# A transformer block with 16 sequences on one core: the last two turns get their own order of dense groups

## What is computed

```python
def _L0_attn_ref(x, Wqkv, bqkv, Wo, bo):
    kqv = (x @ Wqkv + bqkv).reshape(b, s, 3, NUM_HEADS, HEAD_SIZE)   # 16 heads of 32
    ...
    attn = jax.nn.softmax(scores, axis=2)                            # causal
    ...
    return out @ Wo + bo

def _router(x, router_w, e_bias):        # 32 experts, 3 of 8 groups, then 4 of 32 for each token
    ...
def _moe_forward(...):
    topk_idx, topk_w = _router(x, router_w, e_bias)
    # every (token, choice) gets a position within its expert, in token order over all 8192 tokens;
    # positions under C = 320 are kept: slots_token, slots_w
    ...
    Xp = x[slots_token].reshape(E, C, d)                             # 32 experts x 320 tokens
    Y = jnp.einsum('eci,eid->ecd', jax.nn.silu(G) * U, W_down)
    out = jnp.zeros((T, d), x.dtype).at[slots_token].add(Yf)
    shared = jax.nn.silu(x @ shared_gate.T) * (x @ shared_up.T) @ shared_down.T

x = x + _L0_attn_ref(_layernorm(x), ...)
x = x + _L0_ffn_ref(_layernorm(x), ...)
```

## Time and profile before

| what | us |
|---|---|
| median of 3 runs | 2513.14 (2513.05, 2513.14, 2518.89) |
| profiled execution: its time | 2517.61 |
| profiled execution: its span | 2515.8 |
| PE busy in the span | 2311.3 (92%) |
| DVE busy | 1573.3 (63%) |
| ACT busy | 1083.8 (43%) |
| POOL busy | 1110.4 (44%) |

### The profile page before, as it was taken

One profiled execution on the slowest core, in us unless ns is written; L12 is line 12 of the kernel. 1 busy time (PEld: TensorE's weight loads), 2 busy tenths in 40 slices (PEclk: granted clock), 3 DMA queues, 4 the chain that ended last, 5 costly groups with the idle time before them and its releaser, 6 DMA issues. The chain is left out here.

```text
span 2515.8 us, 48721 instructions
## 1 busy us (share of the span) xinstructions
PE 2311.3 (92%) x15466; PEld 1159.8 (46%) x15466; DVE 1573.3 (63%) x4870; ACT 1083.8 (43%) x1849; POOL 1110.4 (44%) x1622
## 2 busy tenths in 40 slices
PE   3789999999999999999999999999998985999997
PEld 1334444444444444444444444444443443666664
DVE  4355666675766666666666666666666564666664
ACT  3344444444343434343434443434443313666664
POOL 1223244434343434444444444444443354777775
PEclk8889999999999999999999999999998897999999
DMA  4212222222222222222222222222212016888886
GB/s 166 68 43 60 53 69 58 67 55 72 57 66 61 65 67 57 66 69 61 60 61 60 60 60 60 60 60 60 62 41 76 10 55 184 230 233 238 236 234 121
DMA packets 180850, 222.52 MB, mean 88 GB/s; under 512 B 37776, under 2 KB 119792, under 8 KB 180624
## 3 DMA queue, kind: packets, MB, share of 16 engines
q1 hardware_dynamic: 154000, 177.58, 23.7%
q0 software_dynamic: 26624, 42.12, 7.5%
HBM read 112.65 MB, written 56.46 MB: 67 GB/s over the span
## 5 line engine op out<-in xcount | busy, mean ns | idle before, releaser
L917 DVE CUSTOM_DVE_ANT_0 junk<-scores,maskrow 128x512 f16<-128x512 f32 (+3 forms) x1024 | 462.5, 487 | 198.2 <-PE scores L524 130.8
L650 ACT ACTIVATE probs<-scores_T 128x512 f32<-128x512 f32 x640 | 369.6, 598 | 215.8 <-PE scores_T L539 212.9
L1033 POOL TENSOR_SCALAR_AFFINE_SELECT probs<-probs 128x256 f32<-128x256 f32 x512 | 192.6, 413 | 380.8 <-ACT probs L650 379.9
L539 PE MATMUL scores_T<-stack_q,stack_k 97*128 97x512 f16 (+3 forms) x1024 | 251.9, 308 | 53.3 <-ACT probs L650 42.7
L1042 POOL DMA_INDIRECT slots_dram<-rec,idx x256 | 258.8, 1011 | 89.0 <-issue 80.1
L524 PE MATMUL scores<-stack_k,stack_q 96*128 96x512 f16 (+3 forms) x1024 | 253.7, 310 | 44.6 <-DVE nmax L917 41.0
L172 PE MATMUL dense<-xT_hi,wqkv_hi 128*128 128x512 f16 x512 | 196.1, 383 | 1.5 <-DVE xT_lo L888 1.5
L173 PE MATMUL dense<-xT_lo,wqkv_hi 128*128 128x512 f16 x512 | 195.0, 381 | 0.0
L174 PE MATMUL dense<-xT_hi,wqkv_lo 128*128 128x512 f16 x512 | 194.9, 381 | 0.0
L1019 POOL TENSOR_TENSOR xres<-xres,bo 128x512 f32<-128x512 f32 x64 | 81.2, 1268 | 247.3 <-DMA xres<-in_x 247.3
L1159 POOL DMA_INDIRECT out<-ex_y,ex_sidx x96 | 153.3, 1597 | 76.6 <-issue 39.1
(11 more groups left out here) (229 smaller groups left out, 5486.2 us busy)
## 6 DMA issues: line engine op xcount, KB each, us to landing
stack_q<-split_q SPq DMA_DIRECT2D x384, 64.0 KB, 2.0
stack_k<-split_k SPq DMA_DIRECT2D x384, 64.0 KB, 2.3
out<-xres SPq DMA_DIRECT2D x67, 256.0 KB, 3.1
xres<-in_x SPq DMA_DIRECT2D x64, 256.0 KB, 2.9
x2n_dram<-x2n SPq DMA_DIRECT2D x16, 1024.0 KB
ex_raw_wg<-in_W_gate SPq DMA_DIRECT2D x32, 512.0 KB, 4.1
ex_raw_wu<-in_W_up SPq DMA_DIRECT2D x32, 512.0 KB, 5.1
ex_raw_wd<-in_W_down SPq DMA_DIRECT2D x32, 512.0 KB, 8.6
```

The lines of the kernel that those rows point to most:

```text
L539: last = pe.matmul(bank[:, at:at + cols], c["stack_k"][0:SROWS + 1, hg, h, kt * P:(kt + 1) * P], c["stack_q"][0:SROWS + 1, hg, h, kt * P:k ...
L650: act.activation(to, at, ACT.Exp, scale=SCALE / (QS * QS)).then_inc(exp_done, 1)
L917: last = dve.tensor_tensor_reduce(out=c["junk"][:, f % 2, at:at + cols], in0=ps["scores"][f % 2][:, at:at + cols], in1=c["maskrow"][:, SEQ ...
L1033: last = pool.affine_select(out=blk, in_=blk, compare_op=ALU.is_ge, fill=0.0, base=0, pattern=[[0, 2], [1, P]], channel_multiplier=-1)
```

## The change

Turns 16 and 17 get lists of their own, `GROUPS_16` and `GROUPS_17`; `Plan` works out for a list the tables that were global before. A group of kind `none` is a number of slots without dense work.

- Turn 16: `out` starts at slot 4, `pos` of sequence 13 stands at slot 24, `x2T` from slot 27, `router` at 35 to 38, and `gate` and `up` from slot 39 on with two or three empty slots after each group, `down` at 92 to 116 likewise. A second `pos` group at slot 63 does sequence 14 in this turn too. The scatters of sequence 13 stand at slots 31 to 61 (every second slot), those of sequence 14 at 74 to 119 (every third).
- Turn 17: `out`, four empty slots, `x2T`, `router`, `gate` and `up` 0 and 1, `pos` of sequence 15 (slot 44), the other `gate` and `up`, `down`. The `ROUTE` steps come three in a slot, from slot 28 on. There is no other `pos` and no scatter within the turn.
- All other turns: the empty slot 93 goes, and the groups behind it stand one slot earlier. The turn keeps 126 slots.

```diff
-          + [(w, j, 4) for j in range(IB - 2) for w in ("gate", "up")]
-          + [("gate", IB - 2, 4), ("pos", 1, 1), ("up", IB - 2, 4)] + [(w, IB - 1, 4) for w in ("gate", "up")]
+          + [(w, j, 4) for j in range(IB) for w in ("gate", "up")]
           + [("xT", 0, 1), ("xT", 1, 1), ("down", 0, 4), ("xT", 2, 1), ("xT", 3, 1)]
...
+GROUPS_16 = ([("none", 0, 4)] + [g for t in range(TT) for g in (("out", t, 4), ("none", 0, 1))] + [("pos", 0, 1), ("none", 0, 2)]
+             + [g for t in range(TT) for g in (("x2T", t, 1), ("none", 0, 1))] + [("router", 0, 4)]
+             + [g for j in range(2) for w in ("gate", "up") for g in ((w, j, 4), ("none", 0, 2))] + [("pos", 1, 1)]
+             + [g for j in range(2, IB) for w in ("gate", "up") for g in ((w, j, 4), ("none", 0, 3))]
+             + [g for t in range(TT) for g in (("down", t, 4), ("none", 0, 3))])
+
+GROUPS_17 = ([("out", t, 4) for t in range(TT)] + [("none", 0, 4)] + [("x2T", t, 1) for t in range(TT)] + [("router", 0, 4)]
+             + [(w, j, 4) for j in range(2) for w in ("gate", "up")] + [("pos", 1, 1)]
+             + [(w, j, 4) for j in range(2, IB) for w in ("gate", "up")] + [("down", t, 4) for t in range(TT)])
...
+class Plan:
+
+    def __init__(self, groups, slots, bias_pace, route_pace, scatters):
+        ends, at = {}, 0
+        for kind, n, pieces in groups:
+            at += pieces
+            ends[kind, n] = at - 1
+        self.groups, self.slots, self.route_pace = groups, max(at, slots), route_pace
+        self.bias = {bias_pace * (t + 1): t for t in range(TT)}
+        self.ln2 = {ends["out", t] + 4: t for t in range(TT)}
+        self.scale2 = {ends["out", t] + 2: t for t in range(TT)}
...
+        self.route_from, self.last_h = ends["router", 0] + 1, ends["up", IB - 1] + 1
+        self.dest_from = {n: ends["pos", n] for n in range(2) if ("pos", n) in ends}
+
+        self.scatter = {slot: (m, n) for m, slots in scatters.items() for n, slot in enumerate(slots)}
...
+PLAN = Plan(GROUPS, 126, 3, 1, {0: range(61, 109, 3)})
+PLAN_16 = Plan(GROUPS_16, 126, 3, 1, {0: range(31, 63, 2), 1: range(74, 122, 3)})
+PLAN_17 = Plan(GROUPS_17, 0, 1, 3, {})
...
-            here, s = (whole or i > 2, i - 3) if n == 0 else (not whole and i == BATCH + 1, i - 2)
+            here, s = whole or i > 2, i - 3 + n
+        elif kind == "none":
+            here, s = False, 0
...
-                    if fin and 0 <= slot - ROUTE_FROM < len(ROUTE):
-                        ROUTE[slot - ROUTE_FROM](i)
+                    if fin and slot >= plan.route_from:
+                        step = (slot - plan.route_from) * plan.route_pace
+                        for route in ROUTE[step:step + plan.route_pace]:
+                            route(i)
...
-                    if (not isinstance(i, int) or i > 2) and slot in SCATTER_SLOT:
-                        scatter(i - 3, SCATTER_SLOT[slot])
+                    if (not isinstance(i, int) or i > 2) and slot in plan.scatter:
+                        m, n = plan.scatter[slot]
+                        scatter(i - 3 + m, n)
```

More of the change, by code:

```diff
@@ L109 @@
 PROBS = 1280
-LN2_SLOT = {last_slot("out", t) + 4: t for t in range(TT)}
 STAT_SLOT = {slot: t for t, slot in enumerate((82, 84, 86, 88))}
 LN1_SLOT = {slot + 5: t for slot, t in STAT_SLOT.items()}
-ROUTE_FROM = last_slot("router", 0) + 1
-DEST_FROM = [last_slot("pos", n) for n in range(2)]
-QLO_SLOT = {last_slot(w, g) + 2: (w, g) for g in range(HG) for w in ("q", "k")}
-LAST_H = last_slot("up", IB - 1) + 1
-BIAS_SLOT = {3 + 3 * t: t for t in range(TT)}
-SCALE2_SLOT = {last_slot("out", t) + 2: t for t in range(TT)}
 SCALE1_SLOT = {slot + 2: t for slot, t in STAT_SLOT.items()}
-SCATTER_SLOT = {slot: n for n, slot in enumerate(range(61, 109, 3))}
 def schedule(i):
@@ L130, in schedule @@
     whole = not isinstance(i, int)
-    for kind, n, pieces in GROUPS:
+    for kind, n, pieces in plan_of(i).groups:
         if kind in PROJ:
@@ L567, in turn @@
             def turn(i, par, proj, attn, fin, nxt):
-                groups, before = schedule(i), before_turn(i)
-                for slot in range(N_SLOTS):
+                plan, groups, before = plan_of(i), schedule(i), before_turn(i)
+                for slot in range(plan.slots):
                     if attn and slot in ST_SLOT:
@@ L658, in turn @@
             def turn(i, par, proj, attn, fin, nxt):
-                groups = schedule(i)
-                for slot in range(N_SLOTS):
+                plan, groups = plan_of(i), schedule(i)
+                for slot in range(plan.slots):
                     if attn and slot in EXP_SLOT:
@@ L665, in turn @@
                         norm1(i + 1, LN1_SLOT[slot])
-                    if fin and slot in LN2_SLOT:
-                        norm2(i - 2, LN2_SLOT[slot])
-                    if fin and slot == LAST_H:
+                    if fin and slot in plan.ln2:
+                        norm2(i - 2, plan.ln2[slot])
+                    if fin and slot == plan.last_h:
                         h_hi(i - 2, IB - 1)
@@ L1047, in turn @@
             def turn(i, par, proj, attn, fin, nxt):
[L1048 removed]
+                plan = plan_of(i)
+                for slot in range(plan.slots):
                     if attn and slot in TRI_SLOT:
                         triangles(i - 1, *TRI_SLOT[slot])
[L1051 to L1056 removed]
+                    if proj and slot in plan.qlo:
+                        qk_lo(i, *plan.qlo[slot])
+                    if fin and slot in plan.bias:
+                        add_bias(i - 2, plan.bias[slot])
+                    if fin and slot in plan.scale2:
+                        scales2(i - 2, plan.scale2[slot])
                     if nxt and slot in SCALE1_SLOT:
                         scales1(i + 1, SCALE1_SLOT[slot])
[L1059 to L1060 removed]
+                    if (not isinstance(i, int) or i > 2) and slot in plan.scatter:
+                        m, n = plan.scatter[slot]
+                        scatter(i - 3 + m, n)
             for t in range(TT):
```

27 lines of the change are left out of this document (8 added, 19 removed).

## The result

The changed kernel takes 2494.34 us (median of 4 runs, 2490.34 to 2497.88) against 2514.64 (4 runs, 2513.05 to 2518.89): ratio 0.9916, 95% interval 0.9894 to 0.9938, so 20.3 us less. Forecast were 2503 and 2498 to 2511. The profiled execution took 2496.56 (before 2517.61), with a span of 2494.5.

The account below looks back on a forecast made before the run. PE bounds the full turns, attention's maxima the first half of turn 16, a chain to the table the end. Tail -12.3 and turn 16 +2.3 give -10.0: 2507.6 profiled, 2503.1 from the median; range 2498 to 2511.

Parts of the forecast that it names:

- The other turns lose a slot without dense work: Turns other than 16 and 17: losing the empty slot put at nothing; 1.4 us in all at a tenth each.
- The only rival about the full turns: Thirteen full turns lose a stall each, over 1.3 us apiece needed to turn -10.0 into +7.5; 2521 or more; chance 0.05.
- full turns of the same length to 0.1 us: Sign expected in the profile after: the full turns of the loop keep their length to 0.1 us.
- signs named for a wrong forecast: Last denominators after 2017 or before 2007, or head group 1's value product waiting over 2 us for late triangles.
- Turn 16: Up to attention's last denominators: added DVE work costs 2.3 us, bounds -0.7 to +7.2; they end at 2011.8.
- A: Tail, start of `out`: most of `down` moves ahead of the last denominators; gain 4.0 us.
- B: Tail, layer norm to router: sequence 14's destinations no longer precede the `xT_lo` copies; gain 3.3 us, bounds nothing to 4.85.
- C: Tail, first `gate` matmul through selection to first scatter: 19.1 us in place of 25.1; gain 6.0.
- D: Tail, 16 scatters on POOL: contention with DVE's `hT_lo` subtractions on shared SBUF interfaces; loss 1.0 us.
- turn 16 gains: Rival: fuller queue cuts DVE's idle time to 2 us, turn 16 is 4 shorter; total -16, 2497; chance 0.13.
- DVE does not keep pace: Rival: idle stays at 9.9 us or a link waits, turn 16 loses 7; total -5, 2508; chance 0.17.

Follow-up runs that it names:

- e7: Kernel before, empty slot and old lists kept, with layer norm 1's statistics four slots earlier: 10.3 us above e5.
- e1: Kernel before with empty slot 93 taken out of the full turns alone, old lists in turns 16 and 17: 13.2 us less.
- e9: Changed kernel with statistics four slots earlier and turn 16 by the old list: 4.8 us more than with both new lists, intervals overlapping.
- e2: Kernel before with the new lists for turns 16 and 17, empty slot 93 kept in the full turns: 0.6 us less, interval 0.9987 to 1.0007.
- e6: Changed kernel run again unaltered, beside the kernel before on one chip: 26.4 us less, median 2513.19 us.
- e8: Kernel before without the full turns' empty slot, plus the new list for turn 17 alone: 2520.99 us, 7.8 above e6.
- e15: Changed kernel with layer norm 1's statistics six slots earlier: no time in the text; the change's own gain was gone.
- e5: Changed kernel with layer norm 1's statistics four slots earlier: 21.5 us below e6, ratio 0.9810 to the kernel before.

## Why the prediction was wrong

**The step that failed** is "The other turns lose a slot without dense work. By the earlier trace rows I put this at nothing". It gave 15.9 us by the start of turn 16. The rows had a hint: one wait of 2.5 us for `probs` (the other of the two is 0.6; further back in the loop it comes in every turn, 27.1 us in ten). I read 5.9 us of waits in 229 as "PE is full". But the end of this wait is not set by PE, so a quarter missing ahead of it lengthens the wait, 0.65 us of the 1.5 that a turn lost. The rest is not assigned: slow stretches behind the wait go along with it, and e7 shows that 0.8 a turn stays when the wait is gone. The only rival about the full turns had another mechanism, a delayed first `scores_T`, and the opposite sign. The forecast "full turns of the same length to 0.1 us" is plainly refuted; e1 shows it without the other parts. Of the signs named for a wrong forecast one came: the last denominators were at 1998.99, before 2007, because of these 15.9 us.

**Turn 16**: a loss of 5.4 us, not 2.3, within its bounds (-0.7 to 7.2). Slot 71 was forecast 71.4 us behind the turn's first `scores_T` and came at 72.2 (1965.26). That this held is in part luck: in the 47.0 us from the first denominators DVE was busy 39.6 and idle 7.4, where I had 41.5 and 5. The rest took 33.7 instead of 31.5: behind its wait of 3.02 PE ran at 1.2 GHz for some 3 us, which loses 1.7 and which my sum did not have. e9 shows that this loss and the tail's gain belong together.

**A**: denominators to the last read of `out` 15.2 (forecast 14.7; 18.7 before): gain 3.5 instead of 4.0. `out` waits for `aT_lo`, as forecast.

**B**: from that read to the first `gate` 8.3 instead of 10.0: gain 1.7, not 3.3. Mis-sized was the way from the last normalised tile to the last `xT_lo`, 3.7 (2018.33 to 2022.07) and not 2.1: ACT's copies `xT_hi` of the earlier tiles wait behind its last normalisation (DVE waits 2.90 for them at 2018.85), and PE 3.08 for the bank.

**C**: gate to first scatter 20.0 (forecast 19.1; 25.1 before): gain 5.1. The selection was done 9.1 behind the gate, forecast 8.5.

**D**: no loss, where I had 1.0. 2042.46 to 2062.15 is 19.69, as before. Two scatters took 1.30 and 1.17 instead of 0.97, 0.5 in all; but before, one of the 16 took 1.49, the same 0.5, which my 1.31 each had in it unseen. The Trainium skill (GPSIMD Engine Reference, Specifications) names a contention with VectorE instructions that have two SBUF inputs. The trace agrees in so far as the subtractions `hT_lo` run beside the three slow scatters, and shows it small.

The sum: forecast -12.3 + 2.3 = -10.0 for the profiled execution, measured -10.4 + 5.4 - 15.9 = -20.9 at the table. Without the full turns it would have been -5.0 (e2, the lists alone, measured 0.6 less), so the forecast was too high for the lists and still too low in all. The rival "turn 16 gains" is refuted. "DVE does not keep pace" came near in size (5 instead of 7), but only in part by its mechanism: from the first denominators to slot 71 DVE's idle time fell from 9.9 to 7.4 us and did not stay, and its work grew from 27.8 to 39.6.

## What to carry to other kernels

Ask of each empty slot or moved instruction which wait comes next behind it on its engine and who sets that wait's end; if another engine does, what is missing ahead of it can be lost, even on an engine that is busy 96% of the time: here 1.5 us a turn for a quarter of 0.65, and 0.28 for the next one. Look at the granted clock behind such a wait too: each slow stretch here lost 1.7 us of full-speed work, though the full turns of e6 and e8, which have fewer of them, were not shorter. Before an instruction is moved earlier, read what the same slot holds on the other engines' queues: four slots earlier gave 21.5 us, and six lost that and the change's own gain.

## What the runs showed that I had not expected

In the groups with e1 to e8, every trace has long idle times of ACT and DVE in turns 15 to 17 that no engine's work explains; the profile says "remote". ACT in e6:

```profile
1863.65 0.60 ACT L641 ACTIVATE glu<-dense 128x512 f32<-128x512 f32 x1 [10.44 <-remote]
```

The first traces of both kernels have none of these, and e9 to e15 have none, though e5 to e8 ran on the same chip as e9 to e15. The kernel before took 2539.6 us there in one group and 2516.4 in the next. The longest, of 9 us and more, lie mostly in the last turns and at the same few instructions. But the loop has some too: in one to seven of its turns DVE's wait of 6.6 to 6.9 us ahead of `denT` is put down to "remote", where it is 5.2 at most in the change's first trace. What they are was not tried and stays open.
